# A gated cross-attention stack on one core: the attention stage's turned groups, score products and rope steps in another order

## The reference

```python
x = x + jnp.tanh(g_xattn[1]) * _L1_xattn_ref(_layernorm(x, axis=-1), ctx_1024, ctx_1024, 16)
...
q = q * cos + rotate_half(q) * sin
k = k * cos + rotate_half(k) * sin
scores = jnp.einsum('bqhd,bkhd->bhqk', q, k) * scale + bias[None]
attn = jax.nn.softmax(scores, axis=-1)
out = jnp.einsum('bhqk,bkhd->bqhd', attn, v)
```

## Time and profile before

| | |
|---|---|
| Time, median of 3 runs | 894.05 us (893.45 to 894.39) |
| Time of the profiled execution | 891.98 us |
| Its span | 889.7 us |
| PE busy | 731.1 us (82%) |
| DVE busy | 709.8 us (80%) |
| ACT busy | 487.5 us (55%) |
| POOL busy | 446.9 us (50%) |

### The profile page before, as it was taken

The page is one execution under the profiler, slowest core; times in us unless marked ns, Lnnn a source line. Parts: engine busy times, 40 slices in busy tenths (PEclk is TensorE's granted clock), DMA queues, the critical chain, the costliest instruction groups (busy, mean ns, idle before and its releaser), DMA issues.

```text
span 889.7 us, 16562 instructions
## 1 busy us (share of the span) xinstructions
PE 731.1 (82%) x5075; PEld 506.9 (57%) x5090; DVE 709.8 (80%) x1228; ACT 487.5 (55%) x936; POOL 446.9 (50%) x328
## 2 busy tenths in 40 slices
PE   0133799999999999878999999999999888878786
PEld 0122778787887877655555666555566432443344
DVE  6864688788888877877989888898887648888985
ACT  1223444444444543324777777777777765555653
POOL 4514565666566654653454554445542015556553
PEclk9965899999999999987999999999999855898999
DMA  7017200000000000000000000000000000001011
GB/s 248 0 54 231 71 1 1 1 1 0 0 0 0 0 1 2 1 0 1 3 2 2 1 1 1 1 1 1 1 1 2 1 1 0 25 24 35 24 36 48
DMA packets 17724, 18.35 MB, mean 21 GB/s; under 512 B 1683, under 2 KB 16916, under 8 KB 17685
## 3 DMA queue, kind: packets, MB, share of 16 engines
q1 hardware_dynamic: 17104, 17.66, 6.2%
q10 hardware_dynamic: 580, 0.20, 0.1%
HBM read 13.39 MB, written 4.19 MB: 20 GB/s over the span
## 4 chain that ended last, share of the span: by engine, by line
PE 46%; DVE 21%; issue 12%; ACT 8%; POOL 4%; DVEq 1%; DMA 1%; POOLq 0%; ACTq 0%; SPq 0%
PE ps_o L626 8%; PE a_ps_t L663 6%; PE a_ps_m L681 6%; DVE maxima L1446 5%; PE a_ps_pv L717 4%; PE a_ps_s L702 3%; DVE f_ps_small L1527 3%; PE ps_gu L597 3%; DVE yscale L1290 2%; PE ps_gu L599 2%; PE ps_gu L598 2%; DVE f_hcode L1543 2%; PE a_ps_pv L725 1%; ACT yn L891 1%; PE f_ps_h L797 1%
## 5 line engine op out<-in xcount | busy, mean ns | idle before, releaser
L1446 DVE TENSOR_REDUCE maxima<-a_ps_m 128x2 f32<-128x512 f32 x256 | 166.3, 686 | 36.8 <-PE a_ps_m L681 36.0
L976 ACT ACTIVATE probs<-a_ps_s 128x512 f32<-128x512 f32 x256 | 149.5, 602 | 44.1 <-PE a_ps_s L702 42.0
L681 PE MATMUL a_ps_m<-stack_t 64*128 64x256 f32 x512 | 107.2, 327 | 17.8 <-DVE maxima L1446 14.6
L681 PEld LDWEIGHTS a_ps_m<-stack_t 64*128 64x128 f32 x512 | 67.9, 187 | 76.1 <-DVE maxima L1446 49.5
L626 PE MATMUL ps_o<-w2t,hqt 128*128 128x256 f32 (+1 forms) x384 | 99.1, 393 | 4.6 <-ACT hqt L912 4.6
L702 PE MATMUL a_ps_s<-stack_t 64*128 64x256 f32 x512 | 100.2, 315 | 3.0 <-DMA stack_t<-neg_max_t 1.9
L1163 POOL TENSOR_TENSOR stack<-roped,stack 128x512 f32<-128x512 f32 x32 | 42.9, 1340 | 116.4 <-DVE stack L1436 114.9
L597 PE MATMUL ps_gu<-w1h,yth 128*128 128x352 f32 x256 | 87.8, 343 | 12.4 <-DVE h L1322 12.4
L717 PE MATMUL a_ps_pv<-probs,v_aug 128*32 128x256 f32 x1024 | 85.3, 406 | 3.0 <-ACT probs L976 2.7
L663 PE MATMUL a_ps_t<-idf,stack 128*128 128x128 f32 x512 | 76.5, 292 | 9.3 <-POOL stack L1163 4.9
L967 ACT CAST stack_t<-a_ps_t 128x512 fp32r<-128x512 f32 x128 | 70.8, 588 | 24.1 <-PE a_ps_t L663 23.2
(11 more groups left out here) (152 smaller groups left out, 1595.3 us busy)
## 6 DMA issues: line engine op xcount, KB each, us to landing
xres<-in_x SPq DMA_DIRECT2D x16, 256.0 KB, 3.2
ctx<-in_ctx SPq DMA_DIRECT2D x16, 256.0 KB, 3.9
out_x<-f_y SPq DMA_DIRECT2D x16, 256.0 KB, 2.1
w_raw<-in_w_gate_up SPq DMA_DIRECT2D x1, 1408.0 KB, 10.6
w_raw<-in_w_fc SPq DMA_DIRECT2D x1, 1024.0 KB, 6.0
w_raw<-in_w_proj SPq DMA_DIRECT2D x1, 1024.0 KB, 12.6
w_raw<-in_w_down SPq DMA_DIRECT2D x1, 704.0 KB, 11.3
stack_t<-neg_max_t SPq DMA_DIRECT2D x32, 8.0 KB
```

The source lines that it names most:

```text
L681: ins = nc.tensor.matmul(a_ps_m[:, half, n, :], a_stack_t[b.par][rows, 0, pair, c * P:(c + 1) * P], a_stack_t[b.par][rows, 1, pair, :], st ...
L976: nc.scalar.activation(a_probs[:, u % 8], a_ps_s[:, u % 2], ACT.Exp).then_inc(a_exp, 1)
L1446: nc.vector.tensor_reduce(a_maxima[:, b.par, c, 4 * quad + half:4 * quad + half + 3:2], a_ps_m[:, half], X, ALU.max).then_inc(a_v_max, 1)
```

## The change

In PE's at_body, at_turn of the next batch is no longer done with six groups in a row at the start. Group 0 stands first, group 1 between the first two score groups, and groups 2 to 7 after every second maxima group up to m = 10. at_turn_out of the batch before now stands behind score groups 0 and 1 instead of between turned groups 1 and 2. Score groups run three ahead, u = m+3, so every maxima group has a score group of the opposite half behind it, and the last three maxima groups have none. ACT's at_body follows the same order. In DVE's at_body, the k rope, the k high part, the norm and the q rope and high part stand between row maxima (after m = 1, 3, 5, 9 and 11); before, the first three stood ahead of at_add_attention and the last two after m = 5 and 8. POOL and SP have the same order as before. The body for the last batch places the lead of the feed-forward stage at other steps. No operation is added or left out.

```diff
--- before.py
+++ after.py
@@ -728,32 +728,31 @@
 
             def at_body(b):
                 nxt = b.shifted(1)
-                for g in range(6):
-                    if g == 2 and b.shifted(-1):
-                        at_turn_out(b.shifted(-1))
-                    if nxt:
-                        at_turn(nxt, g)
-                u = 0
-                for g in range(6, TG):
-                    at_scores(b, u)
-                    if nxt:
-                        at_turn(nxt, g)
-                    u += 1
+                if nxt:
+                    at_turn(nxt, 0)
+                at_scores(b, 0)
+                if nxt:
+                    at_turn(nxt, 1)
+                at_scores(b, 1)
+                if b.shifted(-1):
+                    at_turn_out(b.shifted(-1))
+                at_scores(b, 2)
                 for m in range(MU):
+                    u = m + 3
                     if nxt:
                         at_scores_for_max(nxt, m)
-                    if m % 8 != 7:
+                    if u < SU:
                         at_scores(b, u)
-                        u += 1
-                        if u % 2 == 0 and u >= 4:
-                            at_times_v(b, (u - 4) // 2)
-                    if not nxt and m == 12:
+                    if nxt and m < 12 and m % 2 == 0:
+                        at_turn(nxt, 2 + m // 2)
+                    if m % 2 == 0:
+                        at_times_v(b, m // 2)
+                    if not nxt and m == 10:
                         ff_turn_input(lead[0])
                 if not nxt:
                     pe.wait_ge(a_mt, B)
                     ff_fc(lead[0], 0)
                     ff_fc(lead[0], 1)
-                at_times_v(b, PG - 1)
                 if nxt:
                     at_turn_max(nxt)
 
@@ -990,23 +989,26 @@
             def at_body(b):
                 nxt = b.shifted(1)
                 if nxt:
-                    for g in range(6):
-                        at_turned(nxt, g)
-                for u in range(2):
-                    at_exponent(b, u)
-                    if nxt:
-                        at_turned(nxt, 6 + u)
-                for u in range(2, SU):
-                    at_exponent(b, u)
-                    if u % 4 == 2 and u >= 6:
-                        at_pv_out(b, (u - 6) // 4)
-                    if u == 8 and nxt:
+                    at_turned(nxt, 0)
+                at_exponent(b, 0)
+                if nxt:
+                    at_turned(nxt, 1)
+                at_exponent(b, 1)
+                at_exponent(b, 2)
+                for m in range(MU):
+                    u = m + 3
+                    if u < SU:
+                        at_exponent(b, u)
+                    if nxt and m < 12 and m % 2 == 0:
+                        at_turned(nxt, 2 + m // 2)
+                    if m % 4 == 3:
+                        at_pv_out(b, m // 4)
+                    if m == 12 and nxt:
                         at_v_of(nxt)
-                    if not nxt and u in (3, 7, 11):
-                        ff_norm(lead[u // 4])
-                    if not nxt and u == 14:
+                    if not nxt and m in (1, 4, 9):
+                        ff_norm(lead[m // 4])
+                    if not nxt and m == 12:
                         ff_input_out(lead[0])
-                at_pv_out(b, 3)
                 if nxt:
                     at_max_out(nxt)
 
@@ -1462,20 +1464,23 @@
                                                ALU.mult, ALU.add).then_inc(a_v_out, 1)
 
             def at_body(b):
-                nxt2 = b.shifted(2)
+                nxt, nxt2 = b.shifted(1), b.shifted(2)
                 if nxt2:
                     at_qk_a(nxt2)
-                    at_rope(nxt2, 1)
-                    at_high_part(nxt2, 1)
-                    at_qk_norm(nxt2)
                 if b.shifted(-1):
                     at_add_attention(b.shifted(-1))
                 for m in range(MU):
-                    if b.shifted(1):
-                        at_row_max(b.shifted(1), m)
+                    if nxt:
+                        at_row_max(nxt, m)
+                    if nxt2 and m == 1:
+                        at_rope(nxt2, 1)
+                    if nxt2 and m == 3:
+                        at_high_part(nxt2, 1)
                     if nxt2 and m == 5:
+                        at_qk_norm(nxt2)
+                    if nxt2 and m == 9:
                         at_rope(nxt2, 0)
-                    if nxt2 and m == 8:
+                    if nxt2 and m == 11:
                         at_high_part(nxt2, 0)
 
             def ff_input_stats(b):
```

## The result

| | before | changed |
|---|---|---|
| Time, median | 894.22 us (893.45 to 898.89, 4 runs) | 983.88 us (983.50 to 984.17, 4 runs) |
| Ratio | | 1.099, 95% interval 1.095 to 1.103 |
| Span of the profiled execution | 889.7 us | 981.3 us |
| Turn of maxima to turn of maxima, mean of 15 | 19.62 us | 25.60 us |
| Front, mean of 12 batches (the second to the thirteenth of the 15) | 7.22 us | 9.49 us |

The change costs 89.7 us, about 10%. Front and maxima part are worked out from the records of DVE's row maxima: the front from the end of a batch's last one to the start of the next batch's first, the maxima part from there to its last one's end. Low clock is the time in them in which the granted clock was 0.50, so 1.2 GHz.

A forecast was written before the change was run, and what follows sets the result against it. DVE was taken as nearly the bound in both parts, if kept fed. 14 batches x (4.0 us + 2.7 us clock) = 94 us on the profiled 891.98 gives 986, plus 2 for the median: 988 us, range 942 to 1030.

The forecast's parts named there:

- DMA trip uncovered: Front: first scores wait for the negated maxima through two DMAs, 3.5 us after the last row maximum.
- q_lo, put at nothing: POOL's q_lo for group 0: costed at nothing, since four row maxima (2.6 us) remain after DVE's q high part.
- New front: Last row maximum to next batch's first: steps sum to 7.8 us against 7.5; low clock adds 1.3.
- The wait before denom: Front: DVE idle about 3.7 us before denom in the profile, released by the turn-out.
- Maxima part: Stretch of 16 row maxima: 15.1 us by DVE's work to 16.9 by PE's pace, against 12.3 before.
- PE's end: Upper end of the maxima part: PE needs 2.15 us per two steps, 3.15 with the norm; 16.9 us in all.
- 4.0 us a batch at full clock: Whole batch: middle between 3.1 us more (DVE's lower end) and 4.9 more (PE's upper end).
- Clock: PE's idle front drops the clock for 5 us a batch (a guess), costing 2.7 us: 1.3 front, 1.4 maxima part.
- Rival A: Attention stage: clock stays high, so only 14 x 4.0 = 56 us are lost, 950 us; chance 0.22.
- rival B: Attention stage: clock low for most of each batch, 27 to 34 us a batch, 1000 to 1090 us; chance 0.06.
- The count: Batches affected: moved work in 13, late turn-out in 15, so 14 counted, giving 94 us.
- Rival D: PE paces and the maxima's trip matters to nobody: paired products return 1.6 us a batch, 870 us; chance 0.03.

The follow-up runs named there:

- e3: Changed kernel with turned group 0 made six times instead of once, so PE is busy while the DMAs run; 964.04 us, ratio 1.077.
- e6: Changed kernel with the turn-out ahead of everything, turned group 0 made five times and DVE's order of before; 932.96 us, ratio 1.044.
- e5: Kernel before with only DVE's at_body in the changed order, PE and ACT as before; 933.89 us, ratio 1.044.
- e4: Kernel before with only scores three ahead, so every pair is of opposite halves, groups still in front; 900.58 us, ratio 1.007.
- e8: e7 with scores three ahead, so that all pairs lie in opposite halves; 907.84 us, ratio 1.016.
- e7: Kernel before with turned groups 6 and 7 behind maxima groups 0 and 2, scores two ahead (same half); 915.1 us, ratio 1.023.
- e9: Kernel before with only the turn-out moved behind the second score group; 911.32 us, ratio 1.019.
- e10: Changed kernel with the turn-out ahead of everything and turned group 0 made five times, DVE's order as changed; 958.33 us, ratio 1.072.

## Why the prediction was right, and where its numbers were off

988 us was forecast and 983.88 measured; part of the closeness is luck.

- **DMA trip uncovered.** Right: 3.50 us from last row maximum to first scores in every second steady batch and 3.67 in the others. q_lo, put at nothing, cost nothing: no wait for it stands in the window 430 to 770.
- **New front.** Forecast 7.8 at full clock and 1.3 more at the low one: 9.1; measured 9.49, and 7.8 to 8.0 in the five fronts of e3 at full clock. So the steps were right, and the low clock cost 1.7 us there. The wait before denom was forecast as about 3.7 us; it was 5.2 to 6.2. That figure didn't follow from my own terms: 3.50 + 0.43 + 0.59 + 0.43 to the turn-out and 0.70 to denom are 5.65, less 1.20 of statistics 4.45, which is what e3's fronts at full clock have; the low clock adds to it. The sum of the front used the right terms.
- **Maxima part.** Forecast between 15.1 and 16.9 at full clock, middle 16.0; behind a front of 7.8 us e3 has 15.1 to 15.4. Both ends were mis-sized. DVE's moved work was put at 3.25, with the norm at 1.85 for rstd4 and qn; moved, the two take 0.85, and qn alone 0.74 instead of 1.57. PE's end had 2.15 us per two steps (2.05 measured, mean of the three distances 602.79 to 608.94), and the step with the norm, priced at DVE's 3.15, took 2.35. Neither side alone gives the part (see e6).
- **4.0 us a batch at full clock.** The five batches of e3 without low clock in the front have 23.05 us, 3.5 above the 19.54 of before: 0.5 too high.
- **Clock.** Forecast 5 us low and 2.7 us lost; measured 7.1 us low and 2.3 to 2.7 lost (e3). More time low than assumed, and each us cheaper, so the 2.7 was right by two errors against each other. One came from a misreading: a clock of 0.70 over the 5 us of the earlier trace rows is 3.0 us at 0.50, not 1.5. Nor is the gap all that drops the clock: DVE's order alone does it for 3.70 us a batch (e5), which the forecast didn't have. Rival A (950 us) is excluded by the clock line, rival B by the period.
- **The count.** 14 batches times 6.7 are 94 us; in fact 15 periods times 5.98 are 89.7, and 2.3 behind. An error in the count and one in the term stood against each other. The batch that was read, 19.8 us, is also one of the longer: they alternate between 19.3 and 19.8, and the mean period is 19.62.
- **Rival D**, paired products pay: e4 tests it alone, and they pay nothing while PE isn't the pacer. The Trainium skill was cited for it (TensorEngine Tiling (Array Packing), Theoretical Speedup, up to twofold); the pairs take 0.44 us instead of 0.67, and in e8 against e7, where PE is the pacer, 0.51 us of period come of it.

What the parts cost alone, in us a batch: late turn-out 1.2 (e9), DVE's order 2.55 (e5), spread with pairs 2.36 (e6), the clock 1.7 to 2.7 (e3). They sum to about 8 or more, and the change costs 5.98. Part of the clock is in twice, since e5 has 3.70 us of low clock of its own, and the two orders cover each other in part: 2.8 us together behind the second row maximum, where they cost 1.8 each.

## What to carry to other kernels

Before moving filler work out of a gap, ask which round trip it hid: six turned groups looked like work that could go anywhere, but they covered a DMA, and the engine left idle lost its clock too. Where two engines hand work to each other through a stretch, loading both can cost more than the larger of the two loads and less than their sum (1.8, 1.8 and 2.8 us here), so test each side alone and both together, and compare stretches that start in the same state. Filler that keeps an engine busy through a gap can itself run slowly and hold back what it was to help (e3, e10). A consumer with an in-order queue (here DVE's add) should have its producer placed ahead of the wait that is known to be long, not behind it.

## What the runs showed of the hardware that I had not expected

DVE's norm (qn) depends on what POOL does at the time. It took 411 ns an instruction in e3 and 827 ns in e6, by their groups (window 430 to 690):

```profile
L1417 DVE TENSOR_SCALAR qn<-xres,a_mv,a_rstd 128x256 f32 x20 | 7.4, 411 | 0.4
```

```profile
L1417 DVE TENSOR_SCALAR qn<-xres,a_mv,a_rstd 128x256 f32 x22 | 17.3, 827 | 0.4
```

Timeline of e6:

```profile
565.93 0.69 DVE L1426 TENSOR_TENSOR roped<-part_cos,part_sin 128x512 f32<-128x512 f32 x1
566.08 1.40 POOL L1177 TENSOR_TENSOR a_rstd<-a_var,neg_half 128x2 f32<-128x2 f32 x1 [3.23 <-DVE a_var L1408]
...
567.52 1.30 POOL L1165 TENSOR_TENSOR stack<-roped,stack 128x512 f32<-128x512 f32 x1
567.72 1.57 DVE L1417 TENSOR_SCALAR qn<-xres,a_mv,a_rstd 128x256 f32 x2
```

The first of the two by itself (timeline 567 to 568.88):

```profile
567.72 1.25 DVE L1417 TENSOR_SCALAR qn<-xres,a_mv,a_rstd 128x256 f32 x1
```

Beside POOL's low part (L1165) qn takes 1.57 for two; in the changed kernel POOL was idle ahead of 606.11 and the two took 0.74. The 827 ns are a mean of unlike ones: the first takes 1.25 us and ends 0.15 us after POOL's instruction, the second 0.40, with POOL idle. It is so in all runs, but for the first batch: short with DVE's changed order, long with the old one. It was seen, not tested by itself. The Trainium skill has this in SBUF — State Buffer, Who interferes with whom: DVE and GpSimd share a pair of ports, and a tensor_scalar can be an instruction that wants it. The rows agree: DVE's instruction is long only beside POOL's.

The clock also falls without a gap for a DMA. In e5 it fell nine times between 430 and 690, each time after PE had stood idle for 1.06 to 1.10 us at most at a stretch. Products that nobody needs kept it up in e6 (0.99) and in part in e3 (0.96); e10 has e6's filler and 0.93, and there it fell at the end of each batch's maxima part, after 0.78 us of idle at most.

PE's products in opposite halves don't start strictly in the order of the queue, as was said of every engine above. In the earlier trace rows the first score product starts at 482.08, 0.01 us after the first maxima product and, by the trace, 0.22 us ahead of the second maxima product, which stands before it in the queue.
